# Attention inner step: score and maxima products in one run on TensorE, value products in 512 columns

## The reference

```
x = x + 0.5 * ffn(layernorm(x), ...)      # layernorm, 16-head attention (head width 8), projection, then
                                          # layernorm, top-1 of 8 experts (128 -> 512 -> 128, gelu)
x = x + attn(layernorm(x), ...)           # 16 query heads, 4 key/value heads, rope, softmax(q k / sqrt(8)) v
x = x + 0.5 * ffn(layernorm(x), ...)
```

## Time and profile before

| | |
|---|---|
| three executions | 1610.73, 1616.67, 1618.09 us, median 1616.67 |
| profiled execution | 1616.51 us, of which the span (first to last instruction) is 1614.7 us |
| busy in the span | TensorE 1424.3 us (88%), VectorE 1204.4 (75%), ScalarE 1108.0 (69%), GpSimd 640.4 (40%) |
| granted clock, mean | 0.952 of full speed |
| DMA | 137.60 MB |
| attention passes | about 62 to 470 us and 648 to 1469 us; the rest is opening and experts |

### The profile page before, as it was taken

One profiled execution on the slowest core, in us unless ns is written; L12 is line 12 of the kernel. 1 busy time (PEld: TensorE's weight loads), 2 busy tenths in 40 slices (PEclk: granted clock), 3 DMA queues, 4 the chain that ended last, 5 costly groups with the idle time before them and its releaser, 6 DMA issues.

```text
span 1614.7 us, 35535 instructions
## 1 busy us (share of the span) xinstructions
PE 1424.3 (88%) x12228; PEld 697.2 (43%) x12228; DVE 1204.4 (75%) x2037; ACT 1108.0 (69%) x2056; POOL 640.4 (40%) x972
## 2 busy tenths in 40 slices
PE   2899999999987787899999999999999999999695
PEld 1333433433346774333333333333343333336695
DVE  6788888888834446788888888888888888873343
ACT  1477888787863442678888888888787787776242
POOL 2423345532135444534534443133344552224543
PEclk7699999999998997899999999999999999999798
DMA  4334433442111323433332333333333323201143
GB/s 122 98 99 120 112 103 91 127 103 69 37 39 48 97 72 87 105 99 94 90 78 66 102 93 91 90 79 83 87 91 97 79 70 97 59 25 45 48 116 100
DMA packets 101423, 137.60 MB, mean 85 GB/s; under 512 B 29664, under 2 KB 72032, under 8 KB 101248
## 3 DMA queue, kind: packets, MB, share of 16 engines
q1 hardware_dynamic: 70864, 85.82, 18.6%
q0 software_dynamic: 24000, 45.04, 11.5%
q10 hardware_dynamic: 6384, 4.47, 1.0%
HBM read 79.05 MB, written 53.51 MB: 82 GB/s over the span
## 4 chain that ended last, share of the span: by engine, by line
PE 59%; DVE 28%; issue 6%; DMA 1%; ACT 1%; SPq 1%; POOL 1%; another core or an unknown queue 1%; ACTq 1%; DVEq 1%; POOLq 0%
DVE maxima L1154 23%; PE banks L810 15%; PE banks L798 12%; PE banks L782 11%; PE banks L1491 4%; PE banks L1500 4%; PE banks L837 4%; PE banks L819 3%; PE banks L863 1%; PE banks L844 1%; DVE stats L1231 1%; PE banks L879 1%; DVE split L1162 1%; SPq L445 1%
## 5 line engine op out<-in xcount | busy, mean ns | idle before, releaser
L1154 DVE TENSOR_REDUCE maxima<-banks 128x2 f32<-128x1024 f32 x768 | 924.4, 1223 | 169.5 <-PE banks L782 165.0
L1126 ACT ACTIVATE work<-banks 128x512 f32<-128x512 f32 x1536 | 830.1, 597 | 130.7 <-PE banks L798 117.0
L782 PE MATMUL banks<-K,Q 64*128 64x512 f32 x1536 | 569.9, 460 | 51.2 <-DVE maxima L1154 34.0
L798 PE MATMUL banks<-Q,K 64*128 64x512 f32 x1536 | 569.3, 452 | 11.5 <-ACT work L1126 11.1
L810 PE MATMUL banks<-work,V 128*9 128x256 f32 x6144 | 478.9, 384 | 3.0 <-issue 2.1
L782 PEld LDWEIGHTS banks<-K,Q 64*128 64x128 f32 x1536 | 229.0, 189 | 209.0 <-DVE maxima L1154 118.1
L798 PEld LDWEIGHTS banks<-Q,K 64*128 64x128 f32 x1536 | 229.5, 186 | 194.8 <-issue 158.7
L810 PEld LDWEIGHTS banks<-work,V 128*9 128x9 f32 x6144 | 91.6, 88 | 278.5 <-issue 209.5
L682 POOL TENSOR_TENSOR lo<-full,hi 128x512 fp32r<-128x512 f32 x44 | 56.3, 1280 | 233.5 <-ACT hi L1017 133.1
L1491 PE MATMUL banks<-work 128*128 128x128 f32 x704 | 102.6, 292 | 24.0 <-DVE work L1550 14.5
L1500 PE MATMUL banks<-w,work 128*128 x736 | 108.3, 295 | 14.4 <-DVE work L1555 13.1
(11 more groups left out here) (177 smaller groups left out, 1323.5 us busy)
## 6 DMA issues: line engine op xcount, KB each, us to landing
Q<-q_scratch SPq DMA_DIRECT2D x188, 128.0 KB, 2.6
K<-k_scratch SPq DMA_DIRECT2D x376, 64.0 KB, 2.4
Q<-zero_rows SPq DMA_DIRECT2D x182, 64.0 KB, 2.2
q_scratch<-hi POOLq DMA_DIRECT2D x44, 256.0 KB, 4.7
q_scratch<-lo POOLq DMA_DIRECT2D x44, 256.0 KB, 6.6
k_scratch<-hi POOLq DMA_DIRECT2D x22, 256.0 KB, 4.5
k_scratch<-lo POOLq DMA_DIRECT2D x22, 256.0 KB, 6.4
work<-sorted_x SPq DMA_DIRECT2D x76, 66.0 KB
```

The costliest lines, as they stand in the source:

```text
L782: fill(nc.tensor.matmul(bank, q4[parts(j), n % SLOTS, j // 2, qt * P:(qt + 1) * P], k4[parts(j), n % SLOTS, j // 2, :], start=True, stop=T ...
L798: nc.tensor.matmul(scp[x % EXPS][:, :], k4[parts(j), n % SLOTS, j // 2, kt * P:(kt + 1) * P], q4[parts(j), n % SLOTS, j // 2, :], start=Tr ...
L1126: nc.scalar.activation(prob[:, kt, j ^ 1, :], scp[x % EXPS][:, :], ACT.Exp, scale=SCALE).then_inc(s.probs, 1)
L1154: nc.vector.tensor_reduce(c.maxima[:, at:at + 9:8], c.banks[:, k * S:(k + 2) * S].rearrange("p (m n) -> p m n", m=2), AX.X, ALU.max).then_ ...
```

## The change

The value products are no longer issued in two halves. All eight score and maxima products of a step stand in one run, in the same order as before, and one set of value products with 512 columns follows. The waits of the value products (probabilities of the step before, `out_copied`, the values' bank) stand ahead of that one set. Nothing else changes: banks, plan, VectorE, ScalarE, GpSimd and DMAs keep their instructions and their order.

```diff
-            def weigh(n, kt, half):
-                if half == 0:
-                    pe.wait_ge(s.probs, (n * QT + kt + 1) * J)
-                    if kt == 0:
-                        wait(pe, s.out_copied, n)
-                    if kt == 0 and n % G == 0:
-                        released(pe, "v", n // G)
-                q = slice(half * HALF, (half + 1) * HALF)
+            def weigh(n, kt):
+                pe.wait_ge(s.probs, (n * QT + kt + 1) * J)
+                if kt == 0:
+                    wait(pe, s.out_copied, n)
+                if kt == 0 and n % G == 0:
+                    released(pe, "v", n // G)
                 for j in range(J):
-                    ins = nc.tensor.matmul(outp[32 * j:32 * j + V1, q], v4[:, n // G % VSLOTS, kt, n % G, j, :], prob[:, kt, j, q],
-                                           start=(kt == 0 and half == 0), stop=(kt == QT - 1 and half == 1))
-                if half == 1:
-                    ins.then_inc(s.pv, 1)
+                    ins = nc.tensor.matmul(outp[32 * j:32 * j + V1, :], v4[:, n // G % VSLOTS, kt, n % G, j, :], prob[:, kt, j, :],
+                                           start=(kt == 0), stop=(kt == QT - 1))
+                ins.then_inc(s.pv, 1)
...
                         if half == 0:
                             score(n, kt, j)
-                    if kt:
-                        weigh(n, kt - 1, half)
-                    elif n:
-                        weigh(n - 1, QT - 1, half)
+                if kt:
+                    weigh(n, kt - 1)
+                elif n:
+                    weigh(n - 1, QT - 1)
                 group(n, kt)
```

More of the change, by code:

```diff
@@ L51 @@
 EXPS = 3
-HALF = S // 2
 AHEAD = 2
@@ L976, in main @@
                         step(n, kt)
-                for half in range(2):
-                    weigh(last - 1, QT - 1, half)
+                weigh(last - 1, QT - 1)
             def tail():
```

## The result

The changed kernel took 1654.82 us (median of 4), the kernel before 1613.7 us (median of 4) beside it: 1.0261 times as long, 95% interval 1.0222 to 1.0299. That is +41 us where +80 was forecast, slower as forecast. On a second chip the changed kernel took 1644.9 us and the kernel before 1588.5: 1.0346 (1.0325 to 1.0367), +56 us. The experiments e1 to e8 ran on this second chip, e9 to e12 on another one again.

A forecast was written before the change was run, and what follows sets the result against it. TensorE, with hardly a gap in the second pass, was taken to set the pace, VectorE in places. Terms 98 + 5 + 6 + 5 - 34 = +80 us on 1616.5 us gave 1696 us, range 1655 to 1725 us.

The forecast's parts named there:

- The value set: TensorE's value products: one 512 column set takes 0.98 us, bounds 0.85 and 1.10, saving 0.12 us per step.
- The 92 us: Tiling changes on TensorE: by the drain rule alone, 2 x 0.12 us saved in each of 384 steps; forecast went against it.
- The wait of x(3): Fourth score product waits for exp(0) until 1.27 us; step 2.68 us against 2.43, +98 us over 384 steps.
- Copies and steps without maxima products: ScalarE copies making exp(0) late, +5 and +6 us; 16 steps without maxima products losing about 0.3 us more, +5 us.
- What comes back: TensorE's waits for VectorE before a step, filled by TensorE's own delay: -34 us, bounds 0 and -53.
- the second kind of waits: TensorE waiting for VectorE at the turning of the maxima, 19.1 us in 32 places: counted as giving nothing.
- the first kind: TensorE waiting for VectorE at a step's first maxima product, 34.0 us in 91 places: would vanish.
- the chain of VectorE as fixed: VectorE's work of kt = 3 and kt = 0 stays fixed while TensorE reaches the place 0.5 us later relative to it.
- the second reduction isn't late: VectorE in the new step: second reduction's banks fill 0.6 us after 1.27 us, while the first runs until about 2.07.
- Fewer changes: Rival: x(3) does not wait, TensorE wins 0.1 to 0.2 us in 288 steps, about 1573 us; chance 0.09.
- VectorE wasn't the bound: Rival that VectorE was the bound: nearly every step waits for it, 0.25 us on TensorE hidden, 1616 us; chance 0.05.
- The clock: Rival: TensorE's gaps before x(3) drop its clock to 0.50 in a quarter of the steps, 1777 us; chance 0.05.

The follow-up runs named there:

- e1: Changed kernel with its eight products in one run, but value products as two sets of 256 columns side by side: 1641.3 us, 1.0330 times the kernel before.
- e8: Changed kernel with ScalarE's wait for the value products moved from exp(0) to exp(1) of the step before: 1629.95 us, 1.0262 times the kernel before.
- e9: Kernel before with 128 of the 512 value columns issued once more at the end of each step's second set: 1630.2 us, 1.0263.
- e12: Kernel before, heads 2 and 3's maxima products paired ahead of the first value set, x(2), x(3) behind; one 512 column set at kt = 2: 1610.5 us, 1.0141.
- e4: Changed kernel with exp(0) over 256 of its 512 columns, the rest left as constants: 1594.6 us, 1.0037 times the kernel before.
- e10: Kernel before with exp(0) over 256 of its 512 columns, the rest left as constants: 1590.7 us, 1.0001 times the kernel before.
- e5: Kernel before, unchanged, traced again on the second chip: 1592.1 us (one run).
- e6: Changed kernel, unchanged, timed on the second chip: 1644.9 us, 1.0346 times the kernel before.
- e2: Changed kernel with its single 512 column value set moved between the second and third pair of products in every step: 1655.5 us, 1.0408.
- e7: Kernel before with the last score product x(3) issued twice in each step that has maxima products: 1654.0 us, 1.0402.

## Why the prediction was right in kind and too large

**The value set: right in size, wrong in reason.** 0.98 us, as forecast. But e1 shows that the 0.12 us saved come from having one stretch of value products instead of two, not from 512 columns. The rule that a change of tiling drains the array (TensorEngine Tiling (Array Packing), Key Properties, of the Trainium skill) agrees with e1. The 92 us that I worked out with it were wrong: 0.12 us is what the change to a set and the one back cost together, so that two changes less give 0.12 us per step, 46 us in 384, and the wait took more than that.

**The wait of x(3): right.** x(3) at 1.27 to 1.28 us, 0.42 to 0.43 us to the value products, plain steps of 2.68 us, score products waiting 359 times. e4, e8 and e10 show that it is the cause.

**Copies and steps without maxima products.** On the second chip kt = 1 and kt = 3 steps lose 0.056 and 0.04 us beyond 0.255, 9 us over 184 steps, for the 11 forecast. It is as forecast in kind: 38 steps at kt = 1 and 16 at kt = 3 lose about 0.42 us instead of 0.26; in 28 of them exp(0) stands behind two copies, in 24 behind a scaled one. The 14 other steps lose 0.39 us each, 2 us beyond 0.255, for 5 forecast:

```profile
1485.62 0.73 PE L797 MATMUL banks<-Q,K 64*128 64x512 f32 x3
1486.86 0.49 PE L797 MATMUL banks<-Q,K 64*128 64x512 f32 x1 [0.51 <-ACT work L1121]
```

(here the fourth score product waits 0.51 us). On the first chip these terms are near zero, because the kernel before had lost that time already, around the half clock of the earlier trace rows and in the kt = 1 steps of e5's paragraph. This is 11 of the 15 us between the two chips' results.

**What comes back: the term that was mis-sized.** I counted 34 us, with a bound of 53. On the second chip it is (0.23 + 0.255) us in 92 steps at kt = 0 and (0.255 - 0.15) us in 92 at kt = 2, 54 us. With that the sum is 97 + 9 + 2 - 54 = 54 us, and 54.0 us are measured in the passes; that is the same steps added up and no second proof. Two things were wrong.

I took the second kind of waits, 19.1 us, to stand where the first stood and to give nothing, and the first kind to vanish. Half of the first kind stayed, and most of the second went: on the second chip they fell from 35.2 to 17.3 and from 21.7 to 5.4 us. With 4.6 us at kt = 2 before the turned output, which are gone, the rows have 39 of the 54 us.

And I took the chain of VectorE as fixed. The run issues the last maxima product sooner, 1.27 us after the step instead of 1.55, so the second reduction waits less: the two reductions of a kt = 3 step span 2.36 us in the median instead of 2.47, and the shortest kt = 3 and kt = 0 steps together fell from 6.05 to 5.93 us. I had written that the second reduction isn't late in the new step, which is right, and not seen that it had been late before.

How the other 15 us divide is open. A row's idle time is counted from a modelled end, and understates a wait: in the trace of the changed kernel a group's products (L840, 912.48 for 0.98 us) end at 913.46, and the next product (L781) starts at 913.39 already.

**The rivals.** Fewer changes didn't win, though a set less is worth 0.12 us. VectorE wasn't the bound: plain steps moved by what was forecast. It does pace part of the steps: 54 us of the loss came back there. The clock stayed at 0.99 through a pass, with a gap in each step.

## What to carry to other kernels

Before work is gathered into longer runs, look what lay between a product and the one that reuses its bank. With three banks the fourth of four score products in a row waits for the first one's exponential. A single value set per step of four leaves such a row wherever it stands, unless a group lies in between: at the end of the step x(3) waits (e6), in the middle x(1) of the next (e2). An instruction that holds nothing up itself can still be the cover of a wait, and a second engine's banks are filled only when everything ahead of its products is through.

An addition to one engine's step is worth what it lasts only where that engine paces: the same 0.22 us per step was worth 66 us ahead of the last maxima product (e7) and 40 us behind it (e9).

## What the runs showed of the hardware

Two sets of value products of 256 columns side by side took 0.98 us, the same as one of 512 (e1). An exponential with two waits started 0.62 us after its product (e6), with one 0.56 us at kt = 0 and 2 and 0.60 us at kt = 1 and 3 (e8). VectorE's reductions of 1.22 us follow each other every 1.13 us where both banks are filled (2.35 us for two in the earlier trace rows) and span 2.47 us in plain steps before, where the second waits. The kernel before differed by 1.6% between two chips, by one trace of each 13 us of it outside the passes and 11 us inside, and the ratio of the two kernels by 0.0085.
